# Newton's step for inverse lengths in a local attention stream: its square on ScalarE, the rest later in VectorE's order

## What is computed

```python
l2norm = lambda t: t / jnp.maximum(jnp.linalg.norm(t, axis=-1, keepdims=True), 1e-12)
q = l2norm(q) * qs
k = l2norm(k) * ksc
q = q * cos * scale + rotate_half(q) * sin * scale
k = k * cos * inv + rotate_half(k) * sin * inv
out = local_attention(q, k, v)          # windows of 32, 16 heads of 64
```

## Time and profile before

| What | Value |
|---|---|
| median of 3 runs | 4176.0 us (4174.39 to 4178.6) |
| the profiled execution | 4172.81 us, span 4171.0 us |
| mean granted clock of TensorE | 0.960 |
| busy: TensorE, VectorE, ScalarE, GpSimd | 90%, 83%, 76%, 63% of the span |

### The profile page before, as it was taken

One profiled execution on the slowest core, in us unless ns is written; L12 is line 12 of the kernel. 1 busy time (PEld: TensorE's weight loads), 2 busy tenths in 40 slices (PEclk: granted clock), 3 DMA queues, 4 the chain that ended last, 5 costly groups with the idle time before them and its releaser, 6 DMA issues. The chain is left out here.

```text
span 4171.0 us, 167237 instructions
## 1 busy us (share of the span) xinstructions
PE 3756.9 (90%) x66080; PEld 2932.9 (70%) x66080; DVE 3466.0 (83%) x6851; ACT 3183.2 (76%) x10379; POOL 2641.4 (63%) x2482
## 2 busy tenths in 40 slices
PE   8958969999999999999995877999999999999996
PEld 7937947777777777777773546777777777777773
DVE  2242249999999999999984869999999999999994
ACT  4434438888888888888882666888888888888884
POOL 0000027777777777778761647787777877777771
PEclk9978979999999999999997898999999999999997
DMA  1000013333333343333330003333333333333331
GB/s 39 19 1 24 19 50 109 117 102 118 96 109 116 102 121 95 108 116 104 118 91 8 1 22 99 116 101 119 102 104 116 104 117 105 102 119 100 107 118 34
DMA packets 547031, 361.36 MB, mean 87 GB/s; under 512 B 32321, under 2 KB 532817, under 8 KB 546001
## 3 DMA queue, kind: packets, MB, share of 16 engines
q1 hardware_dynamic: 546256, 350.66, 28.1%
HBM read 248.59 MB, written 101.97 MB: 84 GB/s over the span
## 5 line engine op out<-in xcount | busy, mean ns | idle before, releaser
L1278 POOL TENSOR_TENSOR lt_t<-lt_t 128x512 f32<-128x512 f32 x768 | 973.7, 1289 | 567.1 <-DVE lt_t L1112 567.1
L1014 ACT ACTIVATE lt_pb<-lt_pb,lt_mx 128x64 f32<-128x64 f32 x3072 | 1023.4, 345 | 0.0
L1284 POOL TENSOR_TENSOR lt_t<-lt_t,lt_rn 128x512 f32<-128x512 f32 x768 | 811.0, 1077 | 117.3 <-DVE lt_rn L1140 116.0
L49 PE MATMUL ps<-lt_wh,lt_xh 128*128 128x512 f32 (+1 forms) x1536 | 581.7, 379 | 150.1 <-DVE lt_t L1112 88.8
L1014 ACT ACTIVATION_READ_ACCUMULATOR lt_pb<-lt_pb,lt_mx 128x1 f32 x3072 | 609.3, 198 | 0.0
L996 ACT ACTIVATE lt_qkT<-ps 128x512 f32<-128x512 f32 x768 | 459.1, 598 | 196.8 <-PE ps L816 196.8
L1123 DVE TENSOR_REDUCE lt_ss<-lt_sq 128x8 f32<-128x512 f32 x768 | 518.9, 676 | 14.1 <-ACT lt_sq L991 9.9
L1112 DVE TENSOR_TENSOR lt_t<-ps,lt_tab 128x512 f32<-128x512 f32 x768 | 523.1, 682 | 2.9
L1118 DVE TENSOR_TENSOR lt_t<-ps,lt_tab 128x512 f32<-128x512 f32 x768 | 522.1, 680 | 1.9 <-PE ps L816 0.6
L51 PE MATMUL ps<-lt_wh,lt_xl 128*128 128x512 f32 (+1 forms) x1536 | 523.2, 341 | 0.0
L50 PE MATMUL ps<-lt_wl,lt_xh 128*128 128x512 f32 (+1 forms) x1536 | 522.8, 340 | 0.0
(11 more groups left out here) (213 smaller groups left out, 7653.0 us busy)
## 6 DMA issues: line engine op xcount, KB each, us to landing
lt_vw<-v_scratch SPq DMA_DIRECT2D x768, 256.0 KB, 3.8
v_scratch<-lt_vv SPq DMA_DIRECT2D x384, 256.0 KB, 2.1
lt_wraw<-in_lt_wqkv SPq DMA_DIRECT2D x56, 384.0 KB, 5.8
moe_w<-in_moe_w SPq DMA_DIRECT2D x32, 256.0 KB, 2.8
lt_wo<-in_lt_wo SPq DMA_DIRECT2D x48, 128.0 KB, 3.8
lt_w<-in_lt_w SPq DMA_DIRECT2D x12, 341.0 KB, 4.4
lt_w<-in_lt_w SPq DMA_DIRECT2D x12, 192.0 KB, 4.0
lt_gl<-in_lt_qs SPq DMA_DIRECT2D x2, 768.0 KB, 7.5
```

Source lines behind the costliest of these rows:

```text
L49: nc.tensor.matmul(out, lh, rh, start=start, stop=False)
L1014: ins = nc.scalar.activation(p, p, ACT.Exp, bias=mx[:, par, c:c + 1], accum_out=sm[:, par, c:c + 1])
L1278: nc.gpsimd.tensor_tensor(o, o, t2[:, t, :], ALU.add).then_inc(padd[t], 1)
L1284: nc.gpsimd.tensor_tensor(o, o, rn[:, u[1] % 2, 8 * t:8 * t + 8].unsqueeze(2).to_broadcast([P, 8, DH]), ALU.mult).then_inc(qkd[t], 1)
```

## The change

In the step's queue of ScalarE, `first_guess` gets a third instruction, Square of y0 into ya, with a semaphore of its own (`yad`) and a wait for the Exp before it. `newton` on VectorE loses the instruction that made ya and one wait; yb now waits for `yad`. The call of `newton(u1)` moves from the start of VectorE's slot, behind the maxima, to between `sine(u0, 1)` and `floor(u0)`. The same values are computed.

```diff
-        vmd, lnd, y0d, newt, rnd = [sem("lt_" + n) for n in ("vmd", "lnd", "y0d", "newt", "rnd")]
+        vmd, lnd, y0d, yad, newt, rnd = [sem("lt_" + n) for n in ("vmd", "lnd", "y0d", "yad", "newt", "rnd")]
...
                     nc.scalar.activation(y0[:, par, :], y0[:, par, :], ACT.Exp, scale=-0.5,
                                          bias=res["ln1024"][:, 0:1]).then_inc(y0d, 1)
+                    upto(act, y0d, u)
+                    nc.scalar.activation(ya[:, par, :], y0[:, par, :], ACT.Square).then_inc(yad, 1)
...
                 def newton(u):
                     par = u[1] % 2
-                    upto(dve, y0d, u)
-                    nc.vector.tensor_tensor(ya[:, par, :], y0[:, par, :], y0[:, par, :], ALU.mult).then_inc(newt, 1)
-                    upto(dve, newt, u, 1, 2)
+                    upto(dve, yad, u)
                     nc.vector.tensor_tensor(yb[:, par, :], ya[:, par, :], vm[:, par, :], ALU.mult).then_inc(newt, 1)
-                    upto(dve, newt, u, 2, 2)
+                    upto(dve, newt, u)
...
                     if u3:
                         maxima(u3)
-                    if u1:
-                        newton(u1)
...
                         lengths(u0, 1)
                         sine(u0, 1)
+                    if u1:
+                        newton(u1)
+                    if u0:
                         floor(u0)
```

## The result

The changed kernel takes 4130.6 us, the median of 4 runs (4125.1 to 4135.6), against 4175.2 us (4174.1 to 4178.6) before: a ratio of 0.9892 with a 95% interval of 0.9874 to 0.9909. It is faster by 45 us, as the sign of the forecast had it, and 106 us above the forecast of 4025, beyond the range's upper end of 4110.

A forecast was written before the change was run, and what follows sets the result against it. VectorE paces the stream's 8.20 us step, TensorE close behind. A gain of 0.39 us a step times 384 gives 150 us: 4172.8 - 150 + 3 = 4026, forecast as 4025 us, range 3950 to 4110.

The forecast's parts named there:

- the sign of the forecast: Whole kernel: faster by over 0.2%, chance 0.89.
- ya leaves VectorE, the stalls go, vm is not held: VectorE, per step: ya saves 0.20 us, Newton's stalls 0.87 less 0.15 to 0.2 kept, vm's excess 0.08.
- the sum: VectorE's total gain per step: 0.20 + 0.87 + 0.08 - 0.18 = 0.97 us, if nothing else set the pace.
- Square on ScalarE, hidden: ScalarE, each step: Square adds 0.24 us, to 7.41, hidden under 0.8 to 1.0 us of idle; uncovered, 92 us.
- rn comes later, costed at 0: GpSimd behind rn: rn some 2.4 us later, first addition 1.3 us late, covered; otherwise 0.1 to 0.5 us a step.
- The other six fall from 47.9 to 44.3: Six of eight steps, outside the GELU pair, fall from 47.9 towards TensorE's pace, some 44.3 us.
- Two GELU steps gain nothing: Two of eight steps, 17.5 us: VectorE waits for ScalarE, gains nothing and pays 0.24 us each for Square.
- The third: Rival: ScalarE paces more than two steps, leaving only 0.1 us a step gained, 4138 us; chance 0.07.
- The fifth: Rival: GpSimd's product starts before vm behind rn and holds it 1.04 us; 62 us slower, 4238 us; chance 0.06.
- The watch-list: Profile signs: if right, VectorE idle about 0.7 us a step, TensorE's idle share down; if wrong, possibly an unseen wait.

The follow-up runs named there:

- experiment 8: The changed kernel with one more 128x16 Ln a step added on ScalarE, its result overwritten; 4139.5 us.
- Experiment 4: The changed kernel with GpSimd's weights' product placed between the two additions instead of behind them; 4084.3 us.
- experiment 6: Experiment 4 with the feed-forward part's normalise on VectorE moved from the step's start to behind sine 1, right ahead of Newton's step; 4086.7 us.
- Experiment 7: Experiment 4 with Newton's two instructions and the floor moved ahead of sine 1, behind the second sums; 4059.9 us.
- experiment 12: Experiment 7 with a 128x128 copy added on GpSimd ahead of the weights' product in every step; 4063.8 us.
- experiment 9: The changed kernel with two more passes of 256 columns a step added on TensorE; 4170.4 us.
- Experiments 14 to 16: Square replaces GELU, removing ScalarE's table loads, in the kernel before, the changed kernel and Experiment 7; 4166.1, 4087.3 and 4017.4 us.
- experiment 3: The changed kernel with Newton's two instructions two places earlier, behind the first cosine, with second sums, sine 1 and floor behind; 4174.7 us.

## Why the prediction was right in part, and where it was wrong

**ya leaves VectorE, the stalls go, vm is not held: right.** yb 226 and rn 232 ns lie in the forecast 0.17 to 0.3 us, vm at 167 is undisturbed. VectorE's busy time per step (64.9 steps of 8.09 us in the stretch) is 7.17 us, down 0.79 from 7.96; the sum said 0.97. The shortfall is in part `normalise` (L1179): it meets GpSimd in the change and lasts 1490 ns once in eight steps, against 684 before, 0.10 us a step.

**Square on ScalarE, hidden: right.** ScalarE is busy 7.41 us a step (480.69 / 64.9), the forecast number. In the GELU step it was to cost its 0.24 us; experiment 8 shows such an addition at 9 of 80 us.

**rn comes later, costed at 0: wrong.** This is the first step that failed. It named TensorE's turn and the reuse of t2 as cover, followed GpSimd's round to the two additions, and did not follow it to the instruction behind them. The weights' product (L1291) stands last in that round and feeds TensorE's L856. GpSimd's round of 5.6 us starts with rn, and rn now comes, in the mean, 10.81 us behind its unit's first sums instead of 7.66: 3.15 us later, where 2.4 was written. Experiment 4 takes the product off the end of that round, with rn as late as before: 46 us, and the waits of L856 fall from 19.3 us to none. It also shortens the hold on L1179, and that is worth nothing by experiment 6. Experiment 7 gets 24 us more by an rn that comes 0.8 us sooner (10.01 instead of 10.79), and experiment 12 shows GpSimd off the path then. I take both as the price of the late rn; the 24 us are the sum of two effects, as the floor moves with rn, and no run parts them.

**"The other six fall from 47.9 to 44.3", TensorE's pace: wrong in its size.** This is the second. For steps 2 to 7 I took 6.6 us of a plain step and 4.7 us of feed-forward work, from an estimate of mine where the busy time stood beside it. By the table TensorE was busy 47.33 of their 48.70 us before, 46.45 of 47.68 after, and 46.01 of 46.69 in version 7, where VectorE, GpSimd and the waits were all better. So they end near 46.0 to 46.5, 1.7 to 2.2 us above the 44.3. That TensorE paces there is read from its busy time, and experiment 9 bears it out in part (0.96 of 1.40 us added). The 6.6 us of a plain step were short as well: the earlier trace rows end at 1609.84, 6.75 us, and the 1609.68 of the prediction stands in no row. And 0.8 us of the gap was there from the start: the round before was split into 47.9 and 17.5 us, the latter from ScalarE's squares in one round, where the table has 48.70 and 16.96. The other mistake was an average: TensorE's busy share of the whole round, 7.78 of 8.20, seemed to leave 0.42 us in every step, but more than half of its idle time lay in steps 0 and 1 (1.57 and 0.39 us), where ScalarE's GELU step was to pace by my own forecast, and step 6 was full already.

**"Two GELU steps gain nothing": the mechanism right, the size near.** 16.96 us before, 17.07 after, where 17.5 going to 18.0 was written. Experiments 14 to 16 show that the loads are covered before and count after. The 11.54 and 5.99 us behind the 17.5 were one case; the means of 22 are 12.33 and 6.21, while VectorE's sums start in the mean 3.1 us behind the end of the square ahead of the GELUs and 0.2 us behind the one after them, so that the pair took it 16.96 us. That the step sum came near is in part luck.

So for the round of eight: forecast 44.3 + 18.0 = 62.3 us; version 7 has 46.69 + 16.67 = 63.4; the change 47.68 + 17.07 = 64.75. Of the 106 us missed, 71 lie between the change and version 7 (the late rn), shown by experiments; 35 lie between version 7 and the forecast. For these the table has 2.4 us a round too many in the six steps, made good by 1.3 in the GELU pair; that is an account by busy times, and no edit tests it.

**The rivals.** The third (a little of ScalarE more, 4138) came nearest in time, but not by its mechanism: 80 us more of ScalarE's work cost 9 (experiment 8). The fifth did not happen at the new place. Its hold did in experiment 3, 950 ns where 1.04 us was written, and there it took back the gain, without the 62 us beyond it. The watch-list had VectorE's idle near 0.7 us (0.92) and TensorE's going down (it went from 0.43 to 0.39 us a step, so hardly), and named a wait of sine 1 for GpSimd's additions as the unseen one; it was the weights' product instead. That the two halves of the change give 46 and 38 us alone and 45 together was not foreseen either.

**Open:** why steps 0 and 1 give back only 1.0 of the 2.56 us of the GELU loads, how far below its busy time of 46.0 us TensorE could go in steps 2 to 7, and what holds these steps in version 7 for their last 0.7 us.

## What to carry to other kernels

When a producer moves later in its engine's order, follow its consumer's queue to the end of the round, not to the next two instructions: what pays is the last one in that queue that a full engine waits for, and moving it forward may be worth as much as the change itself. Where the steps of a round differ, read each engine's busy time step by step; a mean idle time is no room where a step is already full. And an instruction order is good only with its partners: the same swap on GpSimd won 46 us on top of the change and lost 295 without it.

## What the chip showed that was not expected

- In the cases shown, a 16-column Vector instruction held by GpSimd ends 0.03 to 0.04 us behind GpSimd's end, and the hold falls on whichever one comes: taking ya away moved it to rn (257 to 649 ns). Such an instruction costs what is left of GpSimd's, up to 1.04 us, and not its own 0.17 us.
- The race behind rn is decided by 0.17 us: the floor starts 0.09 us behind rn, GpSimd's product 0.26 us. With two instructions between them (experiment 3) the floor lasts 950 ns and the kernel is 44 us slower, although rn comes sooner.
- A ScalarE instruction that waits for the one before it starts 0.03 us behind its end (Square behind Exp at 1564.41), so a chain of three small functions takes about 0.8 us of the queue. One more such function (0.2 us a step, 80 us in all) cost the kernel 9 us.
